# Two transformer layers in one kernel: first attention's scores in 32x32 tiles over four banks, its value table as the stationary operand, and scalings moved between engines

## The reference, cut to what matters

```python
# layer 0, first attention: 16 heads of 8 channels, relative keys and values, |distance| clipped at 20
attn = softmax((q @ k^T + q . rel_k[clip(kpos - qpos)]) / sqrt(8))
w    = attn @ v + sum_k attn[q, k] * rel_v[clip(kpos - qpos)]
x    = w @ Wo.T + bo
# layer 0, second part: rmsnorm, attention between the 16 heads of one token, residual, rmsnorm, 8 gated experts
# layer 1: norm, linear attention with a second-order Taylor map (8 heads of 16), residual, norm,
#          router with top 2 of 8 experts plus a shared one (176 hidden)
```

## Time and profile before

| | us |
|---|---|
| median of 3 runs (lowest, highest) | 740.95 (739.88, 742.17) |
| the profiled execution, its own time | 742.6 |
| its span, first to last instruction | 740.8 |
| TensorE busy in the span | 642.9 (87%) |
| VectorE | 546.9 (74%) |
| ScalarE | 385.0 (52%) |
| GpSimd | 145.3 (20%) |
| mean granted TensorE clock | 0.964 |

### The profile page before, as it was taken

One profiled execution on the slowest core, in us unless ns is written; L12 is line 12 of the kernel. 1 busy time (PEld: TensorE's weight loads), 2 busy tenths in 40 slices (PEclk: granted clock), 3 DMA queues, 4 the chain that ended last, 5 costly groups with the idle time before them and its releaser, 6 DMA issues.

```text
span 740.8 us, 16761 instructions
## 1 busy us (share of the span) xinstructions
PE 642.9 (87%) x6432; PEld 514.6 (69%) x6432; DVE 546.9 (74%) x1337; ACT 385.0 (52%) x907; POOL 145.3 (20%) x178
## 2 busy tenths in 40 slices
PE   2687576987999899999998999989998998778987
PEld 1576455765787688777886688768876886456666
DVE  2432587579778986799678986798679967898375
ACT  3375235456646745665655655575566463413532
POOL 2413201330233023300512023301420012001100
PEclk9799679999899999999999999999999999899999
DMA  5502000200110002000110011000200001000000
GB/s 131 226 2 27 11 1 6 26 9 1 15 16 10 1 8 23 15 2 1 23 16 8 1 23 16 9 1 1 29 11 1 1 9 15 1 1 7 2 8 7
DMA packets 75908, 13.43 MB, mean 18 GB/s; under 512 B 69803, under 2 KB 74933, under 8 KB 75701
## 3 DMA queue, kind: packets, MB, share of 16 engines
q1 hardware_dynamic: 73202, 10.78, 8.1%
q0 software_dynamic: 384, 1.05, 0.5%
q10 hardware_dynamic: 2244, 0.55, 0.3%
HBM read 8.95 MB, written 3.16 MB: 16 GB/s over the span
## 4 chain that ended last, share of the span: by engine, by line
PE 40%; issue 25%; DVE 23%; ACT 4%; POOL 3%; DMA 2%; SPq 1%; ACTq 0%; POOLq 0%; DVEq 0%
PE bank L1140 5%; PE bank L1347 4%; DVE prod L876 4%; DVE lg L882 4%; PE bank L1161 4%; PE bank L1348 3%; PE bank L1179 3%; PE bank L1263 3%; DVE nmx L825 3%; PE bank L1203 3%; PE bank L1374 2%; PE bank L1150 2%; DVE at L907 2%; DVE prod L901 2%; PE bank L1376 2%
## 5 line engine op out<-in xcount | busy, mean ns | idle before, releaser
L540 ACT ACTIVATE pm<-bank,nmx 128x256 f32<-128x256 f32 x256 | 100.5, 480 | 67.9 <-DVE nmx L825 67.7
L825 DVE TENSOR_REDUCE nmx<-bank 128x2 f32<-128x512 f32 x128 | 82.2, 684 | 47.7 <-PE bank L1150 47.3
L548 ACT ACTIVATE pT<-bank 128x512 f32<-128x512 f32 x128 | 76.6, 598 | 69.9 <-PE bank L1161 69.5
L1140 PE MATMUL bank<-kT,qbd 64*64 64x256 f32 x1024 | 87.7, 405 | 10.3 <-POOL qr L650 9.6
L1161 PE MATMUL bank<-w,pm 128*128 128x128 f32 x512 | 82.7, 286 | 13.8 <-ACT pm L540 7.2
L605 ACT ACTIVATE ha<-bank,w 128x256 f32<-128x256 f32 x104 | 49.5, 476 | 66.3 <-PE bank L1348 66.3
L1035 DVE SCALAR_TENSOR_TENSOR hu<-bank,w,ha 128x256 f32<-128x256 f32 x104 | 49.9, 481 | 45.9 <-ACT ha L605 45.8
L1179 PE MATMUL bank<-tv,pT 128*128 128x128 f32 (+1 forms) x512 | 81.8, 280 | 1.5 <-ACT rvs L524 1.1
L1179 PEld LDWEIGHTS bank<-tv,pT 128*128 128x128 f32 x512 | 72.1, 196 | 9.8 <-issue 5.9
L1161 PEld LDWEIGHTS bank<-w,pm 128*128 128x128 f32 x512 | 61.1, 147 | 24.8 <-ACT pm L540 14.3
L1347 PE MATMUL bank<-xfT,w 128*128 128x256 f32 x208 | 66.1, 399 | 3.9 <-DVE hu L1035 3.8
(11 more groups left out here) (203 smaller groups left out, 1281.5 us busy)
## 6 DMA issues: line engine op xcount, KB each, us to landing
w<-wpack_dram SPq DMA_DIRECT2D x1, 3944.0 KB, 12.2
xin<-x_in_dram SPq DMA_DIRECT2D x8, 128.0 KB, 2.1
d_qdh<-qdh SPq DMA_DIRECT2D x8, 128.0 KB, 1.8
d_rv<-rvs SPq DMA_DIRECT2D x64, 16.0 KB, 2.2
out_dram<-xo POOLq DMA_DIRECT2D x8, 128.0 KB, 2.3
qc<-d_qdh SPq DMA_DIRECT2D x15, 64.0 KB, 3.8
tv<-d_ev SPq DMA_DIRECT2D x1, 736.0 KB, 4.7
w<-wpack_dram SPq DMA_DIRECT2D x1, 513.0 KB, 4.3
```

The costliest lines, as they stand in the source:

```text
L540: a = act.activation(pm[:, s % 2, c, j], b_s[c][:, j * S:(j + 1) * S], exp, bias=nmx[:, i:i + 1])
L548: act.activation(view(pT, (c * RTC + 2 * s) * C * P, [[1, 2 * C * P]]), b_t[:], copy).then_inc(pT_ready[0], 1)
L825: v.tensor_reduce(nmx[:, i:i + 2], b_s[c][:].rearrange("p (j k) -> p j k", j=2), AX_X, ALU.max, negate=True).then_inc(max_ready[0], 1)
L1140: mm(b_s[c][cols:cols + P // 2, j * S:(j + 1) * S], qbd[rows:rows + P // 2, i], kT[rows:rows + P // 2, t % 2, u], start=True, stop=False, ...
```

## The change

`scores` makes eight tiles in a step instead of four, in four banks (0, 1, 2 and 4), and there are four steps (STEPS) in a batch. `qbd` has 32 columns instead of 64; the key product uses 32 rows and 32 columns of the array, sixteen positions, 32 products a step; the relative product uses 64 rows and 32 columns, eight positions, 32 products a step. Maximum and exponential are now one piece (`weights`) per bank, 16 a batch. The transposes write into the very bank whose scores were exponentiated, so there is no bank of their own. `relative` is one piece per step: the table `tv` (64 columns) is stationary, `pT` is streamed, c=0 and c=1 in the two column halves of the array, and the result goes to bank 0 (bank 1 in the last step), where the next step's transposed weights have just been evicted. VectorE multiplies it by a query mask into `rvm` (four 128x512 instructions a batch), and `weigh` adds it with 16 more products per call, with `fold` as the stationary operand. The DMAs through `d_rv`, `rvs` and `relo` are gone. Several scalings change engine: `xn`, `xl`, `h2` and the copy `v17` to ScalarE; the subtraction in `soft`, the products for `at1` and `o3` and two steps of `rank` to GpSimd, which also gets two small products (`nb`) for each of `xn` and `xl`. All due times are new.

```diff
-QUADS, PER_QUAD = RTC // 2, 6
-HALVES = 2 * QUADS
+STEPS, PER_STEP, AT_ONCE = RTC // 4, 12, 4
+TILES = STEPS * AT_ONCE
...
-        b_s, b_t, b_rv = bank[0:C], bank[2], bank[4]
+        b_s = (bank[0], bank[1], bank[2], bank[4])
...
             def scores(t, s):
-                pe.wait_ge(*raised(exp_ready, t, C * s))
+                pe.wait_ge(*raised(rv_kept, t, s - 1 if s else 0))
+                pe.wait_ge(*raised(pT_ready, t, AT_ONCE * s))
...
                 for j in range(2):
+                    for g in range(AT_ONCE):
+                        odd, c = divmod(g, C)
+                        i = c * RTC + 4 * s + 2 * j + odd
+                        for heads in range(P // MT):
+                            rows, cols = heads * MT, (heads ^ g) * MT
+                            mm(b_s[g][cols:cols + MT, j * S:(j + 1) * S], qbd[rows:rows + MT, i], kT[rows:rows + MT, t % 2, i * QI // KB],
+                               start=j == 0, stop=False, skip_group_check=True, tile_position=(rows, cols))
+                for j in range(2):
+                    for g in (0, 2, 1, 3):
...
+                        for heads in range(P // MT):
+                            rows, own, cols = heads // 2 * P // 2, heads % 2 * MT, (heads ^ g) * MT
+                            a = mm(b_s[g][cols:cols + MT, j * S + lo:j * S + hi], qr[rows:rows + P // 2, i, own:own + MT],
...
             def turn_weights(t, x):
                 pe.wait_ge(*raised(exp_ready, t, x + 1))
-                pe.wait_ge(*raised(pT_ready, t, x))
                 for j in range(2):
                     for kc in range(C):
-                        a = nc.tensor.transpose(b_t[:, ...
+                        a = nc.tensor.transpose(b_s[g][:, ...
...
+            def relative_values(t, s):
+                held = b_s[s // (STEPS - 1)]
+                pe.wait_ge(*raised(pT_ready, t, min(AT_ONCE * (s + 1) + 1, TILES)))
+                for k in range(4 * s, 4 * s + 4):
+                    for c in range(C):
+                        dst = held[c * n:(c + 1) * n, k % 4 * P:(k % 4 + 1) * P]
+                        a = mm(dst, tv[:, v0 * D0:v0 * D0 + n], pT[:, i, c], start=True, stop=not corner,
+                               skip_group_check=True, tile_position=(0, c * n))
...
             def weigh(t, c):
...
+                pe.wait_ge(*raised(rv_kept, t, 4))
+                rows = c * QI * D0
+                for i in range(H0 // PER):
+                    for j in range(PER):
+                        a = mm(b_o[j * MT:(j + 1) * MT, i * P:(i + 1) * P], fold[rows:rows + QI * D0],
+                               view(rvm, own, [[2 * P, RTC // 2], [P + next_own - own, 2], [1, QI]], rows, QI * D0),
+                               start=False, stop=True, skip_group_check=True, tile_position=(rows, j * MT))
...
 # SyncE
-            def relative_out(t):            (eight DMAs to d_rv, three back to relo)
 # VectorE
+                elif name == "keep_rv":
+                    v.tensor_tensor(view(rvm, n * 4 * P, ...), view(b_s[n // (STEPS - 1)], 0, ...), view(own_query, 0, ...), ALU.mult)
...
-                    v.tensor_tensor(on half, b_o, relo, ALU.add);  last: v.tensor_tensor(on, on, rden, ALU.mult)
+                    v.tensor_tensor(on half, b_o, rden half, ALU.mult)
 # GpSimd, norm0 (root1 is alike)
+                    g.tensor_tensor(nb_a[:], mv_a[:, :, 0], minus[:], ALU.mult).then_inc(rstd_a[0], 1)
                     g.tensor_tensor(rs_a[:], ve_a[:], expo[:, 0:C], ALU.pow).then_inc(rstd_a[0], 1)
+                    pool.wait_ge(*raised(rstd_a, t, 2))
+                    g.tensor_tensor(nb_a[:], nb_a[:], rs_a[:], ALU.mult).then_inc(rstd_a[0], 1)
 # ScalarE, scale0 (scale1 is alike, scale2 with Copy and a scale only)
+                    act.activation(dst[:, c], src[:, c], idn, scale=rs[:, c:c + 1], bias=nb[:, c:c + 1])
```

More of the change, by code:

```diff
@@ L235, in build @@
         expo = sb("expo", P, 8)
+        minus = sb("minus", P, C)
         half_root = sb("half_root", P, 1)
@@ L252, in build @@
         v9 = sb("v9", P, 2 * C * V9 + MT)
-        qbd = sb("qbd", P, RT, P // 2)
+        qbd = sb("qbd", P, RT, MT)
         qc = sb("qc", P, RT, D0)
@@ L256, in build @@
         half_mask3 = sb("half_mask3", P, H1 // 2)
[L257 removed]
+        half_mask, quarter_mask = sb("half_mask", P, D0), sb("quarter_mask", P, MT // QI)
         nmx = sb("nmx", P, RT)
[L259 removed]
+        pm = sb("pm", P, AT_ONCE, 2, S)
         pT = sb("pT", P, RT, C, P)
[L261 to L262 removed]
+        rvm = sb("rvm", P, RTC, P)
+        own_query = sb("own_query", P, QI)
+        fold = sb("fold", P, MT)
         oT = sb("oT", P, C, 512)
@@ L387, in expert_bank @@
         def expert_bank(t, n):
-            return b_rv if t == B - 1 and n % 2 else b_a
+            return b_s[3] if t == B - 1 and n % 2 else b_a
         def taylor_bank(t, h):
@@ L441, in rows @@
                     sp.dma_start(*own_rows(half)).then_inc(qc_in[0], 16)
-            def relative_out(t):
-                sp.wait_ge(*raised(rv_kept, t, 4))
-                sp.wait_ge(*raised(on_ready, t, 0))
-                row = RT * QI * D0
-                for q in range(QI):
-                    src = bass.AP(rvs[:].tensor, q * row + (QI - 1 - q) * D0, [[QI * row, H0], [QI * D0, RT], [1, D0]])
-                    sp.dma_start(d_rv.rearrange("r q m d -> q m r d")[q], src).then_inc(rv_out[0], 16)
-                sp.wait_ge(*raised(rv_out, t, 16 * QI))
-                back = d_rv.rearrange("(c r) q m d -> c (r q) (m d)", c=C)
-                sp.dma_start(relo[:, 0], back[0]).then_inc(relo_in[0], 16)
-                for half in range(2):
-                    sp.dma_start(relo[:, 1, half * E // 2:(half + 1) * E // 2], back[1][:, (1 - half) * E // 2:(2 - half) * E // 2]).then_inc(relo_in[0], 16)
             rows(0)
@@ L460, in _ @@
             for t in range(B):
-                if t:
-                    relative_out(t - 1)
                 if t < B - 1:
@@ L467, in _ @@
                     rows(t + 1)
-            relative_out(B - 1)
             sp.wait_ge(stored[0], 16 * B)
@@ L516, in piece @@
                                    copy).then_inc(v_ready[0], 1)
-                elif name == "scores":
+                elif name == "weights":
                     weights(t, n)
@@ L567, in rest @@
                         act.activation(ysq, y[:, c], ACT.Square, accum_out=ss[:, c:c + 1]).then_inc(y_sq[0], 1)
+                elif name == "scale2":
+                    act.wait_ge(*raised(rstd_y, t, 1))
+                    act.wait_ge(*raised(hT_ps, t, 1))
+                    for c in range(C):
+                        a = act.activation(h2[:, c], y[:, c], copy, scale=rs_b[:, 0, c:c + 1])
+                    a.then_inc(h2_ready[0], 1)
                 elif name == "turn2":
@@ L581, in rest @@
                 elif name == "sum3":
+                    act.wait_ge(*raised(v3_ps, t, 1))
+                    for c in range(C):
+                        a = act.activation(view(v17, c * V17, [[D1 + 1, H1], [1, D1]]), view(b_b, c * E, [[D1, H1], [1, D1]]), copy)
+                    a.then_inc(v3_ready[0], 1)
                     act.wait_ge(*raised(vsum_ps, t, 1))
@@ L625, in _ @@
             g.memset(expo[:], -0.5)
+            g.memset(minus[:], -1.0)
             g.memset(half_root[:], 0.5 ** 0.5)
@@ L677, in rest @@
                     g.tensor_tensor(xl[:], xl[:], rbc("fbo", C), ALU.add).then_inc(res_b[0], 1)
+                elif name == "soft":
+                    pool.wait_ge(*raised(l_max, t, 1))
+                    g.tensor_tensor(view(lg, 0, [[H0, C * H0], [1, H0]]), view(lg, 0, [[H0, C * H0], [1, H0]]),
+                                    view(lmx, 0, [[1, C * H0], [0, H0]]), ALU.subtract).then_inc(l_sub[0], 1)
+                elif name == "mix_scale":
+                    pool.wait_ge(*raised(pv_sum, t, 2 * C))
+                    pool.wait_ge(*raised(l_rec, t, 1))
+                    pool.wait_ge(*raised(atT_ps, t, 0))
+                    g.tensor_tensor(view(at1, 0, [[D0, C * H0], [1, D0]]), view(at1, 0, [[D0, C * H0], [1, D0]]),
+                                    view(lsum, 0, [[1, C * H0], [0, D0]]), ALU.mult).then_inc(at_ready[0], 1)
                 elif name == "root2":
@@ L699, in rest @@
                     g.tensor_tensor(rs_c[:], ve_c[:, 0], expo[:, 0:C], ALU.pow).then_inc(rstd_d[0], 1)
+                elif name == "rank":
+                    pool.wait_ge(*raised(sc_steps, t, 5))
+                    g.tensor_tensor(tied[:], tied[:], view(w, W_AT["earlier"][0], [[0, C], [NE, NE], [1, NE]]), ALU.mult).then_inc(sc_steps[0], 1)
+                    pool.wait_ge(*raised(sc_steps, t, 6))
+                    g.tensor_tensor(above[:], above[:], tied[:], ALU.add).then_inc(sc_steps[0], 1)
                 elif name == "store":
@@ L820, in piece @@
                         rel_ends()
-                elif name == "scores":
-                    dve.wait_ge(*raised(s_ps, t, n + 1))
-                    for c in range(C):
```

(22 more changed lines are left out.)

215 lines of the change are left out of this document (92 added, 123 removed), and 85 rows, old and new, of tables (ENGINE_AT, MOVED).

## The result

The changed kernel takes 744.62 us (median, 743.67 to 747.68), the kernel before 740.95 (737.42 to 747.42), nine executions each: ratio 1.0054, 95% interval 1.0030 to 1.0078. Forecast were 711 us, 691 to 735. Medians here are over all executions; the ratios leave out one slow execution of a later run, `r2_before`.

What follows compares the result with a forecast made beforehand. TensorE, 95% busy and taking turns with VectorE, was taken as the main bound. From 742.6 us, five periods 23.0, fill 4.0 and stall 4.2 less, end 1.5 more gave 712.9, or 711 us on the median's basis; range 691 to 735.

Steps and rivals of the forecast that it cites:

- Four steps 8.0: 4.4 us less: Scores on TensorE: four new steps of 2.0 us a batch in place of eight taking 12.4 us.
- rival (d): Scores on TensorE: the sixteen positions don't run at once, 8.2 us more a batch, 802 us; chance 0.03.
- Relative values, 2.8 less: Relative value products on TensorE: 8.4 us a batch falls by 2.8 with two column halves at once.
- TensorE net 5.2 less: TensorE work per batch: scores 4.4 and relative values 2.8 less, weigh 2.0 more, leaving 71.6 us.
- VectorE 2.5 less: VectorE work per batch: 5.3 us removed, 2.8 added by four products out of PSUM, leaving 64.5 us.
- GpSimd 5 to 6 more: GpSimd work per batch: moved operations and nb products add 5 to 6 us on 18, costing latency alone.
- The period is 76.1 to 76.2, 4.6 less: Steady batches: TensorE gives up 5.2 us, hand-overs grow from 3.9 to 4.5; five periods save 23.0 us.
- rival (b): Steady batches: VectorE holds the gain back, only TensorE's full stretch shortens, about 2.3 us a batch, 726 us; chance 0.18.
- rival (c): Scores: a step's chain through one set of banks becomes the bound, period 86.3 us, 776 us in all; chance 0.10.
- Fill and stall, 8.2 less: Start of the kernel: two periods in the fill save 4.0 us, VectorE's vanished wait for relo in batch 0 saves 4.2.
- End +1.5: Behind the last weigh: nb and four moved operations add latency, 1.5 us more, bounds 0 and 4.
- The rule that the prediction weighed: Scores: different row tiles cannot access one PSUM bank simultaneously, which would put a step near 5.3 us.

Runs made afterwards that it cites:

- r2_before: The kernel before with only its due times replaced, by a second search over the order of pieces; 747.69 us (1.008 of the kernel before).
- e_split: The changed kernel with each key product of scores cut in two of 128 keys, twice the instructions for the same columns; 782.23 us (1.057).
- p and d runs: Four runs: the kernel before and the changed kernel, each without the relative scores or with mix over half of the heads; 728.11 to 728.99 us.
- r_after: The changed kernel with only its due times replaced, by a search using durations from its own trace; 731.70 us (0.989 of the kernel before).
- s2_pool: The changed kernel with soft's subtraction, at1, o3 and two steps of rank back on VectorE, due times kept; 783.93 us (1.058).
- s23_both: The changed kernel with the moves to GpSimd and those to ScalarE both undone, back on VectorE, due times kept; 798.1 us (1.077).

## Why the prediction was wrong

- **"Four steps 8.0: 4.4 us less"** was mis-sized. Four steps are 9.84 and eight were 8 x 1.46 = 11.7: 1.8 less (the 0.1 ahead of a step, which I counted before, is left out on both sides). The sixteen positions do run at once, 32 loads within 0.25 us in `e_split`, so rival (d) and the upper bound fall. But I wrote that "issue is far from being the limit" from a step of 16 products, and the new one is 64: after the first 34 weight loads it pauses 0.19 us and then goes on at 16 ns a load. With the 1.04 of the relative part (0.8 forecast) that makes 2.46 for 2.0.
- **Relative values, 2.8 less**: 5.4 us a batch (1.68, 1.02, 1.02 and 1.67) where 38 products of 0.22 were 8.4: 3.0 less, right. **Weigh, 2.0 more**: right. **TensorE net 5.2 less**: by these pieces 2.8, by the busy time 2.1. **VectorE 2.5 less**: 1.9. **GpSimd 5 to 6 more**: 18.0 in eight batches, 2.25 each; its `nb` products take 0.19 to 0.20 us, not up to 1.0.
- **"The period is 76.1 to 76.2, 4.6 less"** is the step that failed most. The sum let 88% of TensorE's saving through because TensorE was 95% busy. The p and d runs show 40 to 50% for either engine in either kernel over the whole time, and 32 to 66% in a period. An estimate from the measured work and these shares, without the stall and the end: 2.8 x 0.45 + 1.9 x 0.45 = 2.1 us a batch, 17 in eight, 724 us: near rival (b)'s 726 by another mechanism, both engines sharing the bound.
- **The order** has no step in the prediction at all. "All due times are new" stood in the change, and I took them as fitting. The other 21 us, from 724 to 744.6, are partly that: 5 to 13 came back by replacing them alone. The rest, 8 to 16 us, stays open; `r_after` may not be the best order, and the shares of the p and d runs were assumed to add.
- **The chain through one set of banks**, rival (c): TensorE never waits for a bank at `scores` in the steady part. It is not the bound there, and its 776 us was wrong; that four large steps are harder to place between the rest would fit the growth of TensorE's idle time, but was only argued.
- **Fill and stall, 8.2 less**: the `relo` stall of 4.19 us went, and the fill still grew by 3.7, so something of about 8 us took its place. The waits show part of it: up to batch 2's `weigh` TensorE stands 17.7 us before the transposes until the exponentials are done, in 12 places, where it stood 13.5 before (7.2 for the exponentials, 6.3 for the one bank of transposes), and 2.7 at `scores` for `keep_rv` and an eviction, both waits of the kind that rival (c) names. In `r_after` the first of these is 10.5 and the fill from batch 0's `weigh` to batch 2's is 135.4 in place of 148.4 with the same work, so there it was the order.
- **End +1.5**: 2.1 behind batch 6's `weigh`. Right.
- **What would show it**: "wrong altogether would be a period above 80". It was 80.55.

## What to carry to other kernels

Before pricing a saving on an engine that is 95% busy in a hand-made order, leave some of its work out and time it: here 40 to 50% came through, on both engines, while work added under the old order came through almost whole, and under a new one to 63%. A change of instructions that brings its own order has to be priced as two changes; replacing the order alone is cheap to try and turned this one from 0.5% slower to 1.1% faster. Small tiles raise the count of instructions as they cut the columns: price both. In the steady part the steps of 128 matmul instructions ran through, most of those of 192 did not.

## What the hardware showed beyond that

- A VectorE instruction of 0.17 us took 6.45 us in `s2_pool`, because eight GpSimd instructions (four rows of two) stood back to back beside it; in three batches of `s2_pool` (6.1 to 6.3 us over the shortest each, 18.5 in all) and three of `s23_both`. VectorE and GpSimd there:

```profile
285.49 1.18 POOL L657 TENSOR_TENSOR qbd<-qT,quarter_mask 128x256 f32<-128x256 f32 x2
285.50 6.45 DVE L1016 TENSOR_TENSOR sc<-sc,ssum 128x16 f32<-128x16 f32 x1
286.63 2.08 POOL L663 TENSOR_TENSOR qr<-qc,half_mask 128x512 f32<-128x512 f32 x2
288.69 1.18 POOL L657 TENSOR_TENSOR qbd<-qT,quarter_mask 128x256 f32<-128x256 f32 x2
289.83 2.09 POOL L663 TENSOR_TENSOR qr<-qc,half_mask 128x512 f32<-128x512 f32 x2
291.99 0.17 DVE L1018 TENSOR_TENSOR bi<-sc,r 128x16 f32<-128x16 f32 x1
```

  It ends when the last of the eight does (285.50 + 6.45 = 291.95, 289.83 + 2.09 = 291.92). The Trainium skill (SBUF — State Buffer, "SBUF: two separate sides") has the rule: a VectorE instruction with two SBUF inputs and a GpSimd one that reads SBUF exclude each other, and whichever starts first keeps the ports for its whole instruction. The trace agrees and adds that the loser does not get in between GpSimd instructions that follow one another.
- Four row tiles of 32 write one bank at once: a bank's tile of 128 rows is filled from all four row positions in one group of sixteen positions, and in `e_split` the first 32 such matmuls start within 0.25 us, each 0.27 to 0.29 long by the trace. The rule that the prediction weighed does not hold here for four row tiles either.
- `relo`'s way through memory, eight small DMAs out and three back, ended 9.5 to 12.3 us behind the end of the last copy into `rvs`, over all batches of the kernel before and of its three reordered forms.
- In a step of 192 short matmul instructions TensorE stopped for 0.6 to 1.5 us with no releaser (`e_split`, 18 times before L1161); the changed kernel, with 128, has no such stop within a step in the steady part, and two, of 0.6 and 0.7 us, ahead of steps in the fill. Whether that is the supply of instructions was not tested.
